# Expert ranks summed by PE from one-hot planes, and layer norms of the second attention applied by ACT

## What is computed

```python
x = x + attn_a(layernorm(x))        # 16 heads, rotary, causal
x = x + ffn(layernorm(x))
x = x + attn_b(layernorm(x))        # one head, scores times a band mask, softmax over all 512
x = x + ffn(layernorm(x))

def layernorm(x, eps=1e-05):
    m = mean(x, -1); v = var(x, -1)
    return (x - m) / sqrt(v + eps)

def ffn(x):
    sel = sigmoid(xf @ expert_sel.T)                 # 4096 x 64
    sel_val, sel_idx = top_k(sel, 4)                 # gates
    out = sum over the 4 experts e of  (relu(xf @ keys[e]) * gate_e) @ values[e]
```

## Time and profile before

| | us |
|---|---|
| median of 3 runs | 1322.15 (1320.84 to 1322.4) |
| profiled execution, device time | 1322.57 |
| its span of instructions | 1320.8 |
| PE busy | 844.6 |
| DVE busy | 806.6 |
| POOL busy | 836.4 |
| ACT busy | 486.4 |

### The profile page before, as it was taken

How to read it: one execution, slowest core, us unless ns; L and a number is a source line. 1 busy time by engine, 2 the same in 40 slices (tenths; PEclk the granted TensorE clock), 3 DMA queues, 4 the chain that set the end, 5 groups by cost and what they waited for, 6 DMA issues and landing times.

```text
span 1320.8 us, 21032 instructions
## 1 busy us (share of the span) xinstructions
PE 844.6 (64%) x6618; PEld 605.7 (46%) x6618; DVE 806.6 (61%) x2325; ACT 486.4 (37%) x1249; POOL 836.4 (63%) x1030
## 2 busy tenths in 40 slices
PE   1889887878788857888866553423387856964100
PEld 0444443333333337888766332313277746964100
DVE  2878988887796145655666774634686753653212
ACT  1177665555555413454433210101134423532000
POOL 6255477866857645479981647547367573996575
PEclk9799998887988757898988665555678877986655
DMA  6856452232443134687553101013025544863322
GB/s 179 279 194 206 160 173 86 90 99 63 142 134 92 59 106 136 179 242 218 153 153 92 41 27 52 35 36 96 23 83 168 156 128 136 240 183 101 101 68 54
DMA packets 206540, 163.71 MB, mean 124 GB/s; under 512 B 15968, under 2 KB 191072, under 8 KB 206432
## 3 DMA queue, kind: packets, MB, share of 16 engines
q1 hardware_dynamic: 185696, 112.00, 29.6%
q0 software_dynamic: 16384, 33.59, 8.2%
q10 hardware_dynamic: 4352, 16.78, 3.3%
HBM read 78.94 MB, written 83.36 MB: 123 GB/s over the span
## 4 chain that ended last, share of the span: by engine, by line
DVE 29%; PE 27%; POOL 19%; issue 11%; another core or an unknown queue 7%; ACT 3%; DMA 2%; SPq 1%; POOLq 0%; DVEq 0%; ACTq 0%
POOL v_aug L1655 9%; PE ps L712 5%; PE ps L721 5%; DVE x_res L1339 3%; PE ps L615 3%; POOL w_attn L1638 3%; PE ps L701 3%; PE ps L574 2%; DVE row_max L1113 2%; POOL sorted_rows L1642 2%; ACT arena L900 2%; SPq L438 1%; POOL arena L1689 1%; POOL xn L1664 1%
## 5 line engine op out<-in xcount | busy, mean ns | idle before, releaser
L1642 POOL DMA_INDIRECT sorted_rows<-xn,dest x256 | 253.4, 990 | 166.9 <-DVE dest L1312 107.4
L1655 POOL DMA_INDIRECT v_aug<-result_rows,dest x256 | 246.1, 961 | 131.5 <-issue 64.9
L900 ACT ACTIVATE arena<-ps 128x512 f32<-128x512 f32 x320 | 183.7, 601 | 107.2 <-PE ps L547 96.4
L712 PE MATMUL ps<-arena 128*128 128x128 f32 x1024 | 155.2, 301 | 53.3 <-DVE arena L1324 30.7
L889 ACT COPY arena<-ps 128x512 f32<-128x512 f32 x128 | 75.0, 586 | 255.1 <-PE ps L721 164.4
L712 PEld LDWEIGHTS ps<-arena 128*128 128x128 f32 x1024 | 141.7, 214 | 58.8 <-DVE arena L1324 32.8
L1324 DVE COPY arena<-ps 128x512 f32<-128x512 f32 x128 | 88.1, 689 | 126.5 <-PE ps L701 68.9
L721 PE MATMUL ps<-arena 128*128 x1024 | 147.8, 291 | 20.8 <-ACT arena L889 16.1
L574 PE MATMUL ps<-arena 64*128 64x128 bf16 (+3 forms) x576 | 130.8, 310 | 38.1 <-DMA arena<-k_parts 18.0
L1113 DVE TENSOR_REDUCE row_max<-ps 128x1 f32<-128x512 f32 (+1 forms) x192 | 127.5, 682 | 44.4 <-PE ps L594 41.3
L721 PEld LDWEIGHTS ps<-arena 128*128 128x128 f32 x1024 | 136.4, 207 | 22.8 <-issue 22.8
(11 more groups left out here) (203 smaller groups left out, 1457.3 us busy)
## 6 DMA issues: line engine op xcount, KB each, us to landing
arena<-sorted_rows SPq DMA_DIRECT2D x128, 256.0 KB
result_rows<-arena SPq DMA_DIRECT2D x128, 256.0 KB
sorted_rows<-arena ACTq DMA_DIRECT2D x16, 1024.0 KB, 4.4
arena<-q_parts SPq DMA_DIRECT2D x16, 512.0 KB
arena<-k_parts SPq DMA_DIRECT2D x16, 512.0 KB
q_parts<-parts SPq DMA_DIRECT2D x52, 128.0 KB, 2.9
k_parts<-parts SPq DMA_DIRECT2D x50, 128.0 KB, 3.1
sorted_rows<-xn,dest POOLq DMA_INDIRECT x256
```

The lines of the kernel that those rows point to most:

```text
L712: mm = pe.matmul(ps[:, e_bank(2, layer, half, n), P * i:P * i + P], ktile[:, v, P * i:P * i + P], xtt[:, v, P * i:P * i + P], start=True, ...
L900: nc.scalar.activation(prob[:, grp % 2, pr % 2, PROB_AT[u]:PROB_AT[u] + T], ps[:, v % 2, :], ACT.Exp, scale=SCALE_A).then_inc(exp_done, 1)
L1642: g.indirect_dma_start(sorted_d[b // HALF][:, :], bass.IndirectOffsetOnAxis(dest[:, 16 * b + n:16 * b + n + 1], 0), xn1[:, b % 2, n // TOP ...
L1655: g.indirect_dma_start(yg[:, b % 2, i // TOPK, C * c:C * c + C], None, result_d[layer][b // HALF][:, :], bass.IndirectOffsetOnAxis(dest[:, ...
```

## The change

Two parts. First, `chosen` and its two adds are gone. `ranks` on PE works on the four choice planes of `one_hot` directly and adds them up in PSUM: 56 matmuls for each batch in place of 14, in both layers, and it waits for `one_hot`.

Second, in attention B the norms are applied by ACT. As `(x - mean) * rs` becomes `rs * x + (-mean * rs)`, DVE computes a column `less_mean = -mean * rs` at the end of the inverse root (one more step of that chain, 128x4), and ACT applies `Identity(scale * x + bias)` with it in four instructions. The norm of `r` stands on ACT behind E and the expert step beside it, that of `nxt` behind the copies of P. The norms of layer 0 stay where they are.

```diff
             def ranks(bank, layer, b):
 
-                pe.wait_ge(msum_done, B * layer + b + 1)
+                pe.wait_ge(oh_done, B * layer + b + 1)
                 for t in range(TT):
-                    o = bank[:, NE * t:NE * t + NE]
-                    pe.matmul(o, tri[:, :], msum[:, t, :], start=True, stop=(t == 0))
-                    for e in range(t):
-                        pe.matmul(o, onesb[:, :], msum[:, e, :], start=False, stop=(e == t - 1))
+                    for e in (t, *range(t)):
+                        for c in range(TOPK):
+                            pe.matmul(bank[:, NE * t:NE * t + NE], tri[:, :] if e == t else onesb[:, :], oh[:, e, c, :],
+                                      start=(e == t and c == 0), stop=(e == max(t - 1, 0) and c == TOPK - 1))
                 for t in range(TT):
-                    mm = pe.matmul(bank[:, NE * TT:NE * TT + NE], onesb[:, :], msum[:, t, :], start=(t == 0), stop=(t == TT - 1))
+                    for c in range(TOPK):
+                        mm = pe.matmul(bank[:, NE * TT:NE * TT + NE], onesb[:, :], oh[:, t, c, :],
+                                       start=(t == 0 and c == 0), stop=(t == TT - 1 and c == TOPK - 1))
                 return mm
...
+            def normed(b, rs, less, rstd, dst, done):
+
+                act.wait_ge(rstd, b + 1)
+                for t in range(TT):
+                    nc.scalar.activation(dst[:, t, :], x[:, TT * b + t, :], ACT.Identity, bias=less[:, t:t + 1],
+                                         scale=rs[:, t:t + 1]).then_inc(done, 1)
+
...
                 attend(it, "E")
                 beside(it, 0)
+                if 0 <= r < B:
+                    before = (1, r - 2) if r >= 2 else (0, B - 2 + r)
+                    act.wait_ge(sent[before[1] // HALF][r % 2], sent_count(*before))
+                    normed(r, rs1, less1, rstd3, xn1[:, r % 2], ln3)
...
                 attend(it, "P23")
                 beside(it, 4)
+                if nxt < B:
+                    if nxt:
+                        bank, n = bjob["XT", it]
+                        act.wait_ge(bank_ready[bank], n + 1)
+                    normed(nxt, rs0, less0, rstd2, xn0, ln2)
                 beside(it, 5)
                 attend(it, "XT")
...
-            def ln_apply(src, mv, rs, dst, b, seq, rstd):
-
-                dve.wait_ge(rstd, b + 1)
-                for t in range(TT):
-                    nc.vector.tensor_scalar(dst[:, t, :], src[:, t, :], mv[:, t, 0:1], rs[:, t:t + 1],
-                                            ALU.subtract, ALU.mult).then_inc(seq, 1)
...
-            def inverse_root(rs, b, seq, rstd):
-
-                q = 3 * ROOT_STEPS * next(roots)
+            def inverse_root(rs, mv, less, b, seq, rstd):
+
+                q = (3 * ROOT_STEPS + 1) * next(roots)
...
-                                                   op0=ALU.add, op1=ALU.mult).then_inc(rstd if last else root_seq, 1)
+                                                   op0=ALU.add, op1=ALU.mult).then_inc(root_seq, 1)
+                dve.wait_ge(root_seq, q + 3 * ROOT_STEPS + 1)
+                nc.vector.scalar_tensor_tensor(out=less[:, :], in0=mv[:, :, 0], scalar=-1.0, in1=rs[:, :],
+                                               op0=ALU.mult, op1=ALU.mult).then_inc(rstd, 1)
...
-            def chosen(b, rank_sem, rank_n):
-
-                dve.wait_ge(oh_done, b + 1)
-                with nc.allow_low_precision(reason="0 and 1 are exact"):
-                    nc.vector.tensor_tensor(two, oh[:, :, 0:2, :], oh[:, :, 2:4, :], ALU.add).then_inc(two_done, 1)
-                    yield 0.6
-                    if b:
-                        dve.wait_ge(rank_sem, rank_n)
-                    dve.wait_ge(two_done, b + 1)
-                    nc.vector.tensor_tensor(msum[:, :, :], two[:, :, 0, :], two[:, :, 1, :], ALU.add).then_inc(msum_done, 1)
-                yield 0.3
```

More of the change, by code:

```diff
@@ L229, in build @@
         slope = sb("root_slope", [P, TT])
+        less0 = sb("less_mean0", [P, TT])
+        less1 = sb("less_mean1", [P, TT])
         xnt = sb("xnt", [P, 2, T + 32])
@@ L254, in build @@
         oh = sb("one_hot", [P, TT, TOPK, NE], BF16)
-        msum = sb("chosen", [P, TT, NE], BF16)
         held = sb("rows_held", [P, 2, NE])
@@ L277, in build @@
         rpos = sb("rank_pos", [P, TT, NE])
-        two = rpos[:, :, :].rearrange("p t e -> p (t e)").bitcast(BF16).rearrange("p (t a e) -> p t a e", t=TT, a=2)
         prods = [v.rearrange("p (t s e) -> p t s e", t=TT, s=TOPK)
@@ L343, in build @@
         oh_done = sem("oh_done")
-        msum_done = sem("msum_done")
-        two_done = sem("two_done")
         pos_seq = sem("pos_seq")
@@ L1024, in _ @@
             for it in range(-1, LAST_IT_B + 1):
+                r, nxt = it - 1, it + 1
                 attend(it, "E")
                 beside(it, 0)
+                if 0 <= r < B:
+                    before = (1, r - 2) if r >= 2 else (0, B - 2 + r)
+                    act.wait_ge(sent[before[1] // HALF][r % 2], sent_count(*before))
+                    normed(r, rs1, less1, rstd3, xn1[:, r % 2], ln3)
                 beside(it, 1)
@@ L1068, in ln_stats @@
                 yield 0.3
-            def ln_apply(src, mv, rs, dst, b, seq, rstd):
-                dve.wait_ge(rstd, b + 1)
-                for t in range(TT):
-                    nc.vector.tensor_scalar(dst[:, t, :], src[:, t, :], mv[:, t, 0:1], rs[:, t:t + 1],
-                                            ALU.subtract, ALU.mult).then_inc(seq, 1)
-                    if t % 2:
-                        yield 0.7
             roots = count()
-            def inverse_root(rs, b, seq, rstd):
-                q = 3 * ROOT_STEPS * next(roots)
+            def inverse_root(rs, mv, less, b, seq, rstd):
+                q = (3 * ROOT_STEPS + 1) * next(roots)
                 dve.wait_ge(seq, 13 * b + 9)
@@ L1376, in route @@
                 yield from choose(b, misc_free, job["LG", b] + 1)
-                yield from chosen(b, misc_ready, job["RK", b - 1] + 1 if b else 0)
             parts_work = route_work = place_work = owner_work = stats1_work = stats0_work = send_work = ()
@@ L1481, in score_out @@
                 finish(ln_stats(x[:, TT * b:TT * b + TT, :], st1, mv1, rs1, b, ln3))
-                inverse_root(rs1, b, ln3, rstd3)
+                inverse_root(rs1, mv1, less1, b, ln3, rstd3)
             def outside_sums(b):
@@ L1503, in combined_stats @@
                 dve.wait_ge(combined, 16 * b + 16)
+                if b:
+                    dve.wait_ge(ln2, 13 * b)
                 finish(ln_stats(x[:, TT * b:TT * b + TT, :], st0, mv0, rs0, b, ln2))
-                inverse_root(rs0, b, ln2, rstd2)
+                inverse_root(rs0, mv0, less0, b, ln2, rstd2)
             def beside(it, place):
@@ L1519, in _ @@
                 beside(b, 0)
-                if route:
-                    before = (1, r - 2) if r >= 2 else (0, B - 2 + r)
-                    dve.wait_ge(sent[before[1] // HALF][r % 2], sent_count(*before))
-                    finish(ln_apply(x[:, TT * r:TT * r + TT, :], mv1, rs1, xn1[:, r % 2], r, ln3, rstd3))
                 beside(b, 1)
@@ L1533, in _ @@
                 beside(b, 4)
-                if prepare:
-                    if nxt:
-                        bank, n = bjob["XT", b]
-                        dve.wait_ge(bank_ready[bank], n + 1)
-                    finish(ln_apply(x[:, TT * nxt:TT * nxt + TT, :], mv0, rs0, xn0, nxt, ln2, rstd2))
                 beside(b, 5)
@@ L1551, in _ @@
                 beside(b, 8)
-                if route:
-                    if r:
-                        bank, n = bjob["RK", r - 1]
-                        finish(chosen(B + r, bank_ready[bank], n + 1))
-                    else:
-                        finish(chosen(B, misc_ready, len(job)))
                 if prepare:
```

## The result

The changed kernel takes 1335.76 us (median of 4 runs, 1335.07 to 1340.13) beside 1322.28 us for the kernel before on the same chip: ratio 1.0114, 95% interval 1.0092 to 1.0137, 13.5 us slower. Forecast was 1326.6, in a range of 1307 to 1338.

A forecast was written before the change was run, and what follows sets the result against it. No engine's total was taken as the bound, so each stage was read alone. Terms -1.4 + 0.4 - 2.3 + 3.6 + 3.0 + 1.2 = +4.5 on 1322.57 us gave 1327.1, or 1326.6 against the median; range 1307 to 1338.

The forecast's parts named there:

- Layer 0: All batches of layer 0: adds gone from DVE, more ranks on PE, -1.4 us, between -5 and +10.
- in the other four: Layer 0 batches other than the two with stalls, 5 and 7: ranks on PE change nothing, 0.
- two stalls at -1.6: Two layer 0 batches where a DVE add was held over 2 us by POOL: -1.6 each, -2.5 at best.
- at most some 24 us: All 16 batches: PE time of the added 42 matmuls, 1.3 or 2.2 us a batch, if nothing hid it.
- The pitch of the ranks: Ranks on PE: 31 ns a matmul at full clock, 51 lower; 56 starts within 1.7 and 3.1 us.
- over 60 ns at full clock: Sign of being wrong: ranks on PE with a pitch above 60 ns at full clock.
- The norms' heads: Layer 1, batches 6 and 7: norm on ACT starts NT 1.9 and 2.5 us later; batches +3.6 and +3.0.
- Batches -1 to 1: Start of layer 1: only `less` in the first two iterations, +0.4; batch 1 waits for POOL's gathers anyway, 0.
- Batches 2 to 5: Layer 1 under POOL's stretches: -1.3 for each of batches 3 and 4, +0.3 for 2, 0 for 5; together -2.3.
- rival 1: ACT's XT copy caught until POOL's stretch ends: batches 3 and 4 both, about 1336; one, 1331; chance 0.14.
- Rival 2: DVE is the bound after all, each us shed counts: -18.8 plus 4 for ranks, about 1307; chance 0.32.
- my reading of rows 11: Batches 2 to 5 under POOL's stream: semaphore waits on DVE or ACT released late, 1.23 us before a root step.

The follow-up runs named there:

- e11: Kernel before with only the ranks' half changed, norms left on DVE, on a chip like the first comparison's: 1315.84 us, ratio 0.9937.
- e6: Kernel before, unchanged, on the 1207 us kind of chip: 1205.95 us, a single run.
- e1: Kernel before with only `ranks` and `chosen` changed, norms left on DVE, on the 1207 us kind of chip: 1191.82 us, ratio 0.9879.
- e7: Kernel before with only the ranks' half changed, run again beside the changed kernel on the 1207 us kind of chip: 1195.7 us, ratio 0.9905.
- e4: Kernel before with the 56 matmuls a batch on PE, both adds still made on DVE but read by nobody: 1207.13 us, ratio 1.0006.
- e3: Kernel before with ranks from the one-hots in layer 0 only, layer 1 keeping adds and norms on DVE: 1194.57 us, ratio 0.9902.
- e5: The changed kernel, unchanged, on the 1207 us kind of chip: 1202.19 us, ratio 0.9944.
- e12: Changed kernel with POOL's short fill of memory between scatters in iterations 2 to 5 too, on a chip like the first: 1298.34 us, ratio 0.9792.

## Why the prediction was right and where it wasn't

The sign was right and the range held the time, but the forecast of +4.5 us is a third of the measured +13.5, and that it came so near is luck: layer 0 was mis-sized by 16 us, batches -1 to 5 of layer 1 by 25, and the two have opposite signs.

**Layer 0, -1.4 taken, -17.7 measured** (-14.9 in e11; between e6 and the other kind's traces -13.3 in e1, -9.9 to -11.9 in five others and -0.3 in e7). The step that failed is "in the other four PE reaches the ranks with no wait for DVE, and positions has other work ahead of it: 0". The adds stood in DVE's list among the row maxima that PE's scores wait for, in every batch; the medians of e4 and e3 price them at about 12.6 us in layer 0, where I had 0.7 us a batch hidden and two stalls at -1.6. And the ranks' own 1.3 us a batch, taken as a cost of +1.3 in batch 5, was none: batch 5 became 3.5 us shorter. Nor does the "at most some 24 us" for all the added matmuls follow from its own prices: 16 times 2.2 is 35; the sum doesn't use it. Busy time on an engine that waits and is waited for by turns was counted at nothing because no wait was seen at one place.

**The pitch of the ranks** was right where nothing disturbs them: 56 in 1.80 us at the upper clock (predicted "within 1.7") and 3.15 at the lower (3.1). It was badly wrong under POOL's stream on the first kind of chip, where three of the 16 batches took 2.7 to 3.0 us and two 8.2 and 10.5, below. The last two are 146 and 187 ns each; the prediction had named over 60 ns at full clock as a sign of being wrong, and the granted clock there was 0.71 and 0.77.

**The norms' heads, right.** NT was predicted 1.9 us later in batch 6 and 2.5 in batch 7; by the distance to `dest` it is 2.3 and 2.8. ACT's four norms took 1.65 us and not 1.2: the exponentials' time (0.44 each) was the nearer row, not the copies. Batch 6 came out at +4.2 (+3.6 taken), batch 7 at +1.7 (+3.0), batch 8 at +0.3 (+1.2). In batch 7 two errors meet: by e11 the ranks' half brought -2.0 there (+0.3 taken) and so the norm cost some 3.7.

**Batches -1 to 1, +0.4 taken, +4.3 measured.** "Batch 1 waits for POOL's gathers in any case: 0" failed. The ranks of batch 1 ran within those gathers and took 10.5 us (0.57 before), and `positions` waited for them:

```profile
729.57 0.22 DVE L1227 TENSOR_TENSOR rows_held<-ps,none_yet 128x64 f32<-128x64 f32 x1 [8.75 <-PE ps L634]
```

That isn't all of it: in e11 the same ranks took 3.73 us, and the stretch is still 2.4 us longer than before.

**Batches 2 to 5, -2.3 taken, +18.7 measured.** This is rival 1, with its mechanism and its place: the XT copies of batches 3 and 4 caught until the stream's end. It was given +3.3 a batch, and the batches came out at +7.8 and +6.5: not only XT's copy but the copy of P ahead of it was held (4.35 us in batch 3), and DVE stood idle for 25 us in both before it could add the attention's output to `x_res`. Of this +2.4 and +0.8 are there in e11 without the norms' move. Batches 2 and 5 lost 1.8 and 2.6 as well, 2.8 in batch 5 of e11 too. The chance given to it, 0.14, was low for the evidence that was there: in batch 5 of before, XT was only half a microsecond later behind its `dest` than in batch 4 (13.2 against 12.7 us), and was held for 34 us, while the change was to move it by 1.9. That its 1336 meets the measured 1335.76 is chance: it left out 16 us of gain in layer 0 and 15 of loss, mostly in batches -1 to 5.

**Rival 2** (DVE's shed work counts, about 1307) had the right mechanism for layer 0, which alone gave more than the -14.8 that it asked for in all (it had put 4 there), and was wrong for layer 1.

The Trainium skill's exclusive lock ("SBUF — State Buffer", section "SBUF: two separate sides") agrees with the traces of the three chips on which kernels with the adds in layer 0 were profiled: nine times the second add met POOL's selects and its add of `x_res`, and it took 2.48 to 2.50 us each time, against a median of 0.29. The 81 ns a pair of "TensorE: Matmul & The Clock Gate" in the Trainium skill is for 128 columns and isn't tested by these pairs of 64, of which 56 in 1.80 us are 32 ns each.

## What to carry to other kernels

When an operation changes engines, ask first what stands before it in the new engine's list: on the 1207 us chips, of two equal norms one was free, and the other reached PE 2 to 3 us late behind the exponentials and cost 3 to 4 where POOL's list didn't hide it; it was cheap again one line earlier. Where two parts of a change touch different stages, time them apart: the ranks alone are faster by 0.6 to 1.2% on both kinds of chip, and only the sum looked like a loss. Where one kernel's trace differs from its own repetition by as much as the effect, take the medians. And where one engine's stream of DMAs holds the others, a chain that comes some microseconds later can lose 5 or more in a batch, and a pause in the stream freed more here than less work beside it.

## What the runs showed of the hardware

Under POOL's unbroken stream of indirect DMAs it isn't waits on semaphores alone that come late. The ranks of batch 6 of layer 0 are 56 matmuls in a row with no wait between them, and on the first chip they took 8.2 us from 455.19 on, while POOL started an indirect DMA every 1.26 us. A part of them:

```profile
456.02 0.22 PE L630 MATMUL ps<-one_hot,onesb 128*128 128x64 bf16 x2
456.92 0.31 PE L630 MATMUL ps<-one_hot,onesb 128*128 128x64 bf16 x5 [0.68 <-issue]
458.35 0.25 PE L630 MATMUL ps<-one_hot,onesb 128*128 128x64 bf16 x3 [1.12 <-issue]
459.08 0.21 PE L630 MATMUL ps<-one_hot,onesb 128*128 128x64 bf16 x1 [0.48 <-issue]
459.79 0.22 PE L630 MATMUL ps<-one_hot,onesb 128*128 128x64 bf16 x1 [0.49 <-issue]
```

The gaps are 0.36 to 1.13 us, the largest near the 1.23 of DVE's root chain in the earlier trace rows. On the chip of e5 the same ranks took 1.95 us, under scatters of the same pitch. So on the first kind of chip the issue of instructions is slowed too, not only the release of a semaphore, and my reading of rows 11 as a price for each wait was too narrow. The Trainium skill, "Runtime: NRT & Kernel Launch", section "Instruction fetch mechanics", says that engines fetch their instructions by DMA in blocks of 256 ahead of time, mostly hidden. Whether the fetch is what suffers here, no run shows; it stays open, as does why the chip of the first comparison and that of e11 and e12 do it (kernel before 1322 and 1324 us) and three others don't (1207 us).
